# Moving the store of each expert unit's result from SyncE's DMA queue to GpSimd's own queue

## The reference

```python
logits = x_flat @ gate_w.T
scores = softmax(logits); topk_ids = top_k(scores, 2)
w = scores * in_topk
gu = einsum('nh,eih->nei', x_flat, experts_gate_up)      # 8 experts, 2 x 704 rows of 512
h = silu(gu[..., :704]) * gu[..., 704:]
expert_out = einsum('nei,ehi->neh', h, experts_down)
out = einsum('neh,ne->nh', expert_out, w)
out = out + sigmoid(x_flat @ shared_expert_gate_w.T) * shared
```

## Time and profile before

| | |
|---|---|
| median of 3 runs | 702.09 us (700.84 to 702.69) |
| profiled execution: time | 701.65 us |
| profiled execution: span of the core | 699.9 us |
| granted TensorE clock, mean | 1.000 of full speed |
| TensorE busy | 689.2 us, 98% of the span |
| expert units | about 551 to 697 us of the span |

### The profile page before, as it was taken

The page is one execution under the profiler, slowest core; times in us unless marked ns, Lnnn a source line. Parts: engine busy times, 40 slices in busy tenths (PEclk is TensorE's granted clock), DMA queues, the critical chain, the costliest instruction groups (busy, mean ns, idle before and its releaser), DMA issues.

```text
span 699.9 us, 9941 instructions
## 1 busy us (share of the span) xinstructions
PE 689.2 (98%) x3229; PEld 570.5 (82%) x3229; DVE 556.8 (80%) x713; ACT 337.2 (48%) x451; POOL 196.8 (28%) x144
## 2 busy tenths in 40 slices
PE   7999999999999999999999999999999999999997
PEld 6888888888888788888888888888888888888875
DVE  6588887778979998899996753769434798999897
ACT  4322222222245565566663333742233588888872
POOL 4344444544440000000000000426785111211244
PEclk9999999999999999999999999999999999999999
DMA  8056667767642236433210511614200799999974
GB/s 306 12 165 210 225 217 243 245 222 242 222 156 91 90 121 251 169 102 108 90 61 0 229 58 65 242 44 164 104 2 2 280 359 377 391 379 393 386 299 150
DMA packets 38686, 130.70 MB, mean 187 GB/s; under 512 B 6658, under 2 KB 10756, under 8 KB 35588
## 3 DMA queue, kind: packets, MB, share of 16 engines
q1 hardware_dynamic: 35828, 124.45, 49.6%
q0 software_dynamic: 1536, 4.20, 1.9%
q10 hardware_dynamic: 1296, 1.71, 0.7%
HBM read 120.89 MB, written 9.46 MB: 186 GB/s over the span
## 4 chain that ended last, share of the span: by engine, by line
PE 95%; DVE 3%; issue 1%; ACT 1%; DMA 0%; DVEq 0%
PE ps L929 25%; PE ps L896 8%; PE ps L892 8%; PE ps L893 8%; PE ps L1151 5%; PE ps L828 5%; PE ps L830 5%; PE ps L829 5%; PE ps L1121 4%; PE ps L1130 4%; PE ps L1132 3%; PE ps L1131 3%; PE ps L1056 1%; PE ps L1138 1%; PE ps L812 1%
## 5 line engine op out<-in xcount | busy, mean ns | idle before, releaser
L431 POOL TENSOR_TENSOR c_lo<-ring,c_hi 128x512 fp32r<-128x512 f32 x64 | 85.1, 1330 | 101.9 <-ACT c_hi L549 101.9
L549 ACT ACTIVATE c_hi<-ring 128x512 fp32r<-128x512 f32 x64 | 40.4, 633 | 128.1 <-PE ps L896 101.0
L892 PE MATMUL ps<-qk_hi,c_hi 128*128 128x512 f32 x256 | 100.2, 391 | 0.1
L436 POOL TENSOR_TENSOR w_lo<-raw,w_hi 128x1024 fp32r<-128x1024 f32 x11 | 26.7, 2429 | 259.7 <-ACT w_hi L677 245.7
L893 PE MATMUL ps<-qk_lo,c_hi 128*128 128x512 f32 x256 | 99.6, 389 | 0.0
L1316 DVE TENSOR_TENSOR runmax<-runmax,att 128x512 f32<-128x512 f32 x64 | 90.6, 1416 | 6.0 <-DVE att L1310 3.2
L896 PE MATMUL ps<-qk_hi,c_lo 128*128 128x512 f32 x256 | 68.5, 389 | 0.0
L1310 DVE SCALAR_TENSOR_TENSOR att<-ring,beta,ps 128x512 f32 (+1 forms) x64 | 47.8, 747 | 24.2 <-PE ps L896 23.5
L929 PE MATMUL ps<-p_hi,d_hi 128*128 128x512 f32 x256 | 64.2, 393 | 0.1
L929 PE MATMUL ps<-p_hi,d_lo 128*128 128x512 f32 x256 | 63.2, 389 | 0.0
L929 PE MATMUL ps<-p_lo,d_hi 128*128 128x512 f32 x256 | 63.2, 389 | 0.0
(11 more groups left out here) (307 smaller groups left out, 1498.4 us busy)
## 6 DMA issues: line engine op xcount, KB each, us to landing
ring<-stream SPq DMA_DIRECT2D x64, 512.0 KB, 4.0
raw_u<-up_in SPq DMA_DIRECT2D x22, 1024.0 KB, 6.9
raw_d<-down_in SPq DMA_DIRECT2D x33, 512.0 KB, 7.3
ring<-ctx_in SPq DMA_DIRECT2D x32, 512.0 KB, 3.3
raw<-shared_in SPq DMA_DIRECT2D x11, 768.0 KB, 4.5
raw_u<-up_last_in SPq DMA_DIRECT2D x11, 768.0 KB, 6.7
slots<-blank SPq DMA_DIRECT2D x15, 256.0 KB
late<-wqkv_in SPq DMA_DIRECT2D x1, 3072.0 KB, 10.7
```

Source lines behind the costliest of these rows:

```text
L431: pool.tensor_tensor(c_lo[:, s % 2, :], ring1[:, s, 0, :], c_hi[:, s % 2, :].bitcast(F32), ALU.subtract).then_inc(lo1_ready, 1)
L549: act.activation(c_hi[:, s % 2, :], ring1[:, s, 0, :], ACT.Copy).then_inc(hi1_ready, 1)
L892: pe.matmul(ps[:, s, :], hi, qk_hi[:, k, :], start=(k == 0), stop=False)
```

## The change

In SyncE's program the wait for `y_ready` and the store go. In GpSimd's program they stand at the head of the loop over units, ahead of the subtraction. The semaphores, the buffer, the rows of `slots` and the bytes are the same; iteration e of GpSimd's loop stores the result of unit e - 1, and e runs from 1 to `final` - 1, which are the same nine results.

```diff
@@ load_unit, SyncE @@
                 load_up(u, expert_, 1)
                 load_up(u, expert_, 2)
-                if not second:
-                    sp.wait_ge(y_ready, u - 1)
-                    sp.dma_start(slots[bass.ds((u - 2) * P, P), :], y_out[:, :]).then_inc(y_stored, 16)
                 load_down(u, expert_, 0)
                 load_down(u, expert_, 1)
@@ GpSimd @@
             with pool.Fori(1, final) as e:
+                pool.wait_ge(y_ready, e)
+                pool.dma_start(slots[bass.ds((e - 1) * P, P), :], y_out[:, :]).then_inc(y_stored, 16)
                 down_last_low(e)
             pool.wait_ge(y_stored, (final - 1) * 16)
```

## The result

| | before | after |
|---|---|---|
| median, beside each other | 702.39 us, 6 runs (700.84 to 704.20) | 706.29 us, 6 runs (704.74 to 706.95) |
| ratio, 95% interval | | 1.0052 [1.0039, 1.0065] |
| profiled execution, time and span | 701.65, 699.9 us | 706.57, 705.0 us |
| mean granted clock | 1.000 | 0.997 |

The time is 3.9 us longer in this comparison, outside the range on record (700.4 to 705.0).

The account below looks back on a forecast made before the run. It took TensorE's matmuls to bound the expert units (12.77 us each), with DMA just below. Zero for SyncE, GpSimd, order and gathers left 701.65 profiled, 702.1 us median; own range 700.8 to 703.0, 8-in-10 range 700.4 to 705.0.

Parts of the forecast that it names:

- SyncE's part: Expert units: dropping SyncE's wait and store issue saves 0, between 0 and -0.17 us a unit.
- GpSimd's wait: Expert units: the wait ends at 577.44, leaving 5.3 us of idle time before GpSimd's subtraction, so it costs 0.
- GpSimd's issue: Expert units: each store's issue takes 1 to 2.5 us, judged from indirect DMAs, all covered by 5.3 us; cost 0.
- The order of transfers: Expert units: the store's new place among weight loads costs 0, between -0.1 and +0.10 us a store.
- The gathers: Behind the units: gathers wait for the last store; taken as 0, with 0 to +2.1 us possible.
- The slower rival: Expert units: weights beside GpSimd's store land later, chiefly the first up piece; 705.6 or 708.7 us, chance 0.15.

Follow-up runs that it names:

- e1: The kernel before, unchanged, run again as a kernel of its own: 702.67 us, ratio 1.0001.
- e5: The kernel before with only the wait for y_ready added to GpSimd's loop, the store still on SyncE: 702.03 us, ratio 0.9996.
- e6: The kernel before with one small direct DMA of GpSimd added behind the gathers: 702.71 us, ratio 1.0018, two of ten runs above 706.
- e7: The kernel after with its nine stores left out, GpSimd counting up their semaphore itself: 702.28 us, ratio 1.0000.
- e13: The kernel before with four one-column memsets added at the head of GpSimd's program: 702.73 us, ratio 1.0008.
- e10: The kernel before with two small direct DMAs of GpSimd, looped with a register address, behind the gathers: 702.82 us, ratio 1.0016.
- e9: The kernel after, unchanged, run a second time: 702.96 us, ratio 1.0010, three of twelve runs lost the tie.
- e14: The kernel after, unchanged, run a third time: 704.30 us, ratio 1.0022, six of twelve runs lost the tie.
- e2: The kernel after plus a guard: GpSimd waits for VectorE's product before its subtraction for shared tile 1; 702.84 us, ratio 1.0003.

## Why the prediction was wrong

**What held**, by its own steps:

- SyncE's part at 0: the next down load is issued at 583.28, 1.13 us behind the last up piece (582.15); in the earlier trace rows it was 1.15. As predicted, VectorE's subtraction decides that, not the store. SyncE's wait for it went from 18.9 to 24.0 us and nothing moved.
- GpSimd's wait covered: its row of waits is

```profile
POOL slots L494 <- ACT y_out L704: 51.2, 9, 5.7
ACT wu_hi L686 <- DMA raw_u<-up_in: 1.8, 3, 1.1
```

and behind each store 4.05 us or more of idle time are left ahead of the subtraction.
- GpSimd's issue was mis-sized: 0.56 us (0.61 at most), not 1 to 2.5. A direct store isn't like an indirect one; SyncE's 0.36 was the nearer row. Nothing hung on it.
- The order of transfers at 0: ScalarE's wait for up weights is 1.8 us for 1.3 in the earlier trace rows, and the store lands after 6.2 to 7.8 us. The page's queues after:

```profile
q1 hardware_dynamic: 34532, 122.09, 48.7%
q0 software_dynamic: 2256, 6.56, 2.6%
```

Against the earlier trace rows q0 gained 2.36 MB for 0.026 x 705.0 - 0.019 x 699.9 = 5.0 us of all engines, or 2.1 us for each MB: cheaper than the 3.17 that I took from indirect DMAs, and than SyncE's 2.79. The shares have one decimal only, which makes it 1.8 to 2.4; SyncE's figure is a mean over the whole kernel, so the two are not for the same load.
- The gathers at 0: the first is at 680.72, 2.71 us behind the last mark; in the earlier trace rows and the mark at 672.93 it is 2.70.
- The slower rival (weights land later, from 705.6 up) gave a time near the measured one, but it isn't what happened: the units lost nothing.

**What failed** is a step that the prediction never wrote down as one. Its sum is "0 for SyncE, 0 for GpSimd, 0 for the order, 0 for the gathers", all of them in and behind the expert units, on top of 701.65 us. For the 550 us ahead of them it has no term: it took them as given, since no instruction there is changed, with no row to show that they take the same time in every execution. One thing in them is a tie whose loser costs 3.5 us by the medians (702.57 to 706.11), and the change alters how often it is lost, through the program of GpSimd and not through the work.

The price can be read from two marks, the start of VectorE's product and GpSimd's first subtraction in the units. Between them are 107.36 or 107.37 us in all six profiles that won with no guard (before, e1, e5, e6, e7, e13). The lost tie without a drop of the clock is e10's, with it e9's, here their first marks in the units and e10's window:

```profile
559.90 2.42 POOL L485 TENSOR_TENSOR wd_lo<-raw_d,wd_hi 128x1024 fp32r<-128x1024 f32 x1 [21.72 <-DVE wu_lo L1643]
454.00:456.00 2.00, 2.00 (x20) 2.00 (x19) 1.64 (x6) 1.81 (x4) 0.00 (x0) 1.00 0.50 111
...
561.23 2.43 POOL L481 TENSOR_TENSOR wd_lo<-raw_d,wd_hi 128x1024 fp32r<-128x1024 f32 x1 [21.71 <-DVE wu_lo L1637]
```

e10 has 559.90 - 450.35 = 109.55 us, so 2.2 us for the wait. e9 has 561.23 - 450.04 = 111.19, e14 111.15 and the profile after 562.15 - 451.01 = 111.14, so 3.8 us with the drop, and 1.6 of them for the clock. The windows after say the same: 2 x (0.30 + 0.50 + 0.06) = 1.7 us of full speed are missing. The 4.95 us ahead of the first mark are thus 1.17 of a late start, which the unchanged kernel has too in e1, and 3.78 of the lost tie.

That the measured median lies outside the range is partly luck: all six runs of the first comparison lost, where half of all do. The same kernel's medians in e9 (702.96) and e14 (704.30) lie inside the range, and the missing term would have stayed unseen.

The trace before did show the place: two rows 0.01 us apart on the two engines that share a port, the short one on the way to TensorE's next rows. The prediction had even read an issue of 2.47 us for 0.95 beside VectorE's subtractions in the gathers. With a rival "the tie is lost in some of the runs" at 706, the range would have reached beyond 705.

**Stays open:** what in GpSimd's program tilts the tie. Both sides go back to one point. TensorE's first result of self attention releases VectorE at 444.38 before and 445.54 after, and VectorE then works without idle time up to the product, 5.46 and 5.47 us later. GpSimd waits for TensorE's last result there (`y_psum`), and its first iota begins 4.66 and 4.67 us behind the same point; three iotas on comes the subtraction. That is why it is a tie in every execution, early or late. Nothing shows what differs: in the profile after GpSimd's iota begins 0.17 us behind VectorE's operation on `x` (450.21 and 450.04), and it does before too (449.04 and 448.87). In nanoseconds the packed trace has VectorE's product ahead of GpSimd's subtraction by 1 to 4 in the four lost ties (after, e9, e10, e14) and by 1 to 18 in the six won ones, so the recorded starts don't tell who gets through. Without the guard, a direct DMA of GpSimd anywhere in the program goes with losses (20 of 50 runs, against 1 of 163), the wait alone (e5), the missing stores (e7) and a late start (e13) don't. Whether its code, its queue's set-up or something else decides it by less than the records resolve wasn't tried. Nor was it shown why six runs in a row lost in the first comparison and 3 and 6 of 12 later. Why the clock didn't drop in e10, behind the same idle time as in the others, stays open too.

No version here beats both kernels. The kernel after with the guard (e2) has the store moved and the tie safe, at 702.84 with an interval that holds 1.

## What to carry to other kernels

Compare the two traces by marks, stage by stage, before explaining a difference by the stage that was changed: here 4.95 of 5.1 us lay ahead of it, 3.78 of them about 100 us ahead. In a kernel written by hand for each engine, look for places where a short VectorE operation and a long GpSimd operation on SBUF start within some hundredths of a microsecond with TensorE behind them; a semaphore that orders them cost 0.2 us here and takes a gamble out of every later measurement. And look at the single runs: a median between two clusters (702.6 and 706.1) says how often something happened, not how long the kernel takes.

## What the runs showed that I had not expected

- A VectorE operation of one column took 0.16 or 2.36 to 2.37 us by the outcome of a tie with GpSimd within 0.02 us.
- 2.06 us of idle TensorE cost some 1.6 us more through the granted clock (0.70, 0.50, 0.94 after it), and in e10 the same idle time was followed by 1.00 in every window and cost nothing more.
- The first record of the full clock begins 6.63 us into the span in one execution of the kernel before and 11.42 in another (e1), which puts the rest 1.3 us later (first transposes 0.65 or 1.11 us).
- GpSimd's issue of a direct store of 256 KB took 0.56 us in a stage where VectorE was 88 to 94% busy, while its indirect DMAs beside VectorE's subtractions took up to 2.87 us.
